# Layer 0 one slot behind its chunk's landing instead of two, in a fused two-layer graph network

## The reference, cut to what matters

```
o = sum over v in 1..3 of (adj == v) @ (x @ w_v);  x = layernorm(x + o + bias)
h = x @ W.T + b;  e = leaky_relu(h @ we1 + be1 + (h @ we2 + be2).T, 0.01)
attention = softmax(where(adj > 0, e, -9e15), axis=1)
x = layernorm(x + attention @ h)
```

## Time and profile before

| | |
|---|---|
| median of 3 | 1608.69 us |
| the profiled execution | 1608.2 us |
| its span | 1606.5 us |
| its mean granted TensorE clock | 0.969 |
| VectorE, ScalarE busy | 1088.5, 979.4 us |

### The profile page before, as it was taken

How to read it: one execution, slowest core, us unless ns; L and a number is a source line. 1 busy time by engine, 2 the same in 40 slices (tenths; PEclk the granted TensorE clock), 3 DMA queues, 4 the chain that set the end, 5 groups by cost and what they waited for, 6 DMA issues and landing times.

```text
span 1606.5 us, 19366 instructions
## 1 busy us (share of the span) xinstructions
PE 1435.4 (89%) x6934; PEld 668.8 (42%) x6934; DVE 1088.5 (68%) x2432; ACT 979.4 (61%) x1536; POOL 119.5 (7%) x154
## 2 busy tenths in 40 slices
PE   1747798889999999999999988999999989998996
PEld 0323344344444444444444433444444444444443
DVE  3556677867878968778678665666566766666554
ACT  2223535555556556456555467787787887788674
POOL 3101111110101110100101030000000000000000
PEclk9988899899999999999999998999999999999998
DMA  9999999995889879967969121000000001000100
GB/s 117 125 123 118 126 98 118 112 115 69 97 108 98 98 70 121 86 69 96 84 67 115 13 66 40 8 27 27 27 27 27 27 27 52 28 27 27 34 1 15
DMA packets 124164, 109.60 MB, mean 68 GB/s; under 512 B 4960, under 2 KB 115104, under 8 KB 124064
## 3 DMA queue, kind: packets, MB, share of 16 engines
q0 software_dynamic: 67584, 67.12, 45.7%
q1 hardware_dynamic: 56480, 41.20, 9.1%
HBM read 296.49 MB, written 13.14 MB: 193 GB/s over the span
## 4 chain that ended last, share of the span: by engine, by line
PE 56%; ACT 17%; DVE 12%; DMA 11%; issue 4%; SPq 0%; DVEq 0%; ACTq 0%
PE ps L1208 35%; PE ps L1167 18%; ACT neg_masks L991 13%; DMA edges<-x 7%; DVE neg_masks L597 3%; DVE pos_masks L599 2%; DMA x_rows<-x 2%; PE ps L1176 1%; DMA e_scratch<-e_turned 1%; DMA e_row<-e_scratch 1%; PE ps L1222 1%; DVE tables L660 1%; ACT L1049 1%; PE ps L1188 1%; DVE seen L559 1%
## 5 line engine op out<-in xcount | busy, mean ns | idle before, releaser
L991 ACT ACTIVATE neg_masks<-e_row,cols 128x512 int8<-128x512 f32 x1024 | 640.4, 708 | 176.7 <-PE ps L1208 137.6
L1208 PE MATMUL ps<-pos_masks,tables 128*128 128x512 fp8e4 x2048 | 616.1, 383 | 65.6 <-DVE pos_masks L599 55.7
L1208 PE MATMUL ps<-neg_masks,tables 128*128 128x512 fp8e4 x2048 | 615.2, 382 | 0.0
L1167 PE MATMUL ps<-edge_masks,tables 128*128 128x512 fp8e4 (+1 forms) x2048 | 470.7, 389 | 0.0
L1208 PEld LDWEIGHTS ps<-pos_masks,tables 128*128 128x128 f16 x2048 | 197.1, 98 | 322.4 <-issue 93.3
L597 DVE TENSOR_TENSOR neg_masks<-pos_masks,neg_masks 128x2048 uint16<-128x2048 uint16 x128 | 156.9, 1226 | 241.9 <-ACT neg_masks L991 240.5
L1208 PEld LDWEIGHTS ps<-neg_masks,tables 128*128 128x128 f16 x2048 | 201.7, 98 | 246.8 <-issue 8.8
L1167 PEld LDWEIGHTS ps<-edge_masks,tables 128*128 128x128 f16 x2048 | 203.3, 100 | 238.1 <-issue 22.2
L578 DVE TENSOR_SCALAR edge_masks<-edges 128x512 uint16<-128x512 uint16 x512 | 123.5, 307 | 77.6 <-PE ps L1167 77.6
L982 ACT ACTIVATE edges<-ps 128x1024 uint8<-128x1024 bf16 x64 | 65.0, 1016 | 177.1 <-PE ps L1176 177.1
L599 DVE TENSOR_TENSOR pos_masks<-pos_masks,neg_masks 128x2048 uint16<-128x2048 uint16 x128 | 156.8, 1225 | 4.4
(11 more groups left out here) (128 smaller groups left out, 728.5 us busy)
## 6 DMA issues: line engine op xcount, KB each, us to landing
adj_in<-adj POOLq DMA_DIRECT2D x84, 512.0 KB, 12.0
tables<-adj POOLq DMA_DIRECT2D x28, 512.0 KB, 20.9
e_row<-e_scratch SPq DMA_DIRECT2D x34, 256.0 KB, 4.1
edges<-adj POOLq DMA_DIRECT2D x16, 512.0 KB, 12.0
part_scratch<-a_c_rows SPq DMA_DIRECT2D x18, 256.0 KB, 3.3
part_in<-part_scratch SPq DMA_DIRECT2D x18, 256.0 KB, 3.0
edges<-x SPq DMA_DIRECT2D x8, 512.0 KB, 16.2
x_rows<-x SPq DMA_DIRECT2D x8, 512.0 KB, 4.9
```

What stands on the lines that cost most here:

```text
L991: ins = e.activation(GN[:, n:n + GR].bitcast(I8), e1row[:, q % 2, :], ACT.Sign, bias=t2[:, JC * c + j:JC * c + j + 1])
L1167: ins = e.matmul(ps[:, h, :], v_hl[:, i, JC * c + j, :], U0[:, n:n + GR].bitcast(kind), start=c == 0 and j == 0 and i == 0, stop=c == NCH ...
L1208: ins = e.matmul(z_bank(q, k), tab[:, c, 2 * k + i, j, :], mask[:, n:n + GR].bitcast(F8A), start=first and j == 0 and i == 0, stop=final a ...
```

## The change

START goes from 5 to 4, so every batch sits one slot earlier, and a tail's offsets are one larger in the same slot. TensorE does layer 0 of chunk k-1 in slot k instead of k-2. A batch that isn't fresh comes first in TensorE's slot, a fresh one after layer 0 as before. In VectorE's slot the masks of a batch that isn't fresh stay near the front, the edge masks of chunk k-1 go ahead of packing, and fresh masks go behind it, behind statistics and e_sums. ScalarE's, GpSimd's and SyncE's code isn't edited (but for `fresh`, which moves out of ScalarE's block); what they do in a tail follows the offsets. The tables of parts 4 to 6 (AGAIN, slots 64 to 66 and two behind) keep their slots. There are 148 slots.

```
-START = 5
+START = 4
...
+def fresh(m):
+
+    return SLOTS[m] == NCH * (BATCH[m][1] // 2 + 1) + START
...
-            return [(S, k - 8 * (S + 1)) for S in range(NS) if 0 <= k - 8 * (S + 1) < 8]
+            return [(S, k - 8 * (S + 1) + 1) for S in range(NS) if 0 <= k - 8 * (S + 1) + 1 < 8]
...
                 for m in at(k):
-                    masks(m)
-                    after(m)
+                    if not fresh(m):
+                        masks(m)
+                        after(m)
+                if 1 <= k <= NCH:
+                    split_rest(k - 1)
+                if 1 <= k <= K:
+                    edge_masks(k - 1, 0)
+                    edge_masks(k - 1, 1)
...
-                if 1 <= k <= NCH:
-                    split_rest(k - 1)
                 if k < K:
                     check_and_pack(k)
                 for S, off in tails(k):
                     if off == 2:
                         v_of(S, 1)
-                if 1 <= k <= K:
-                    edge_masks(k - 1, 0)
-                for S, off in tails(k):
-                    if off == 2:
                         statistics(S)
                     if off == 3:
                         e_sums(S)
-                if 1 <= k <= K:
-                    edge_masks(k - 1, 1)
+                for m in at(k):
+                    if fresh(m):
+                        masks(m)
+                        after(m)
...
-                if 2 <= k < K + 2:
-                    layer0(k - 2, 0)
+                for m in at(k):
+                    if not fresh(m):
+                        batch(m)
+                        after(m)
+                if 1 <= k < K + 1:
+                    layer0(k - 1, 0)
                 for S, off in tails(k):
                     if off == 2:
                         o_of(S, 1)
-                if 2 <= k < K + 2:
-                    layer0(k - 2, 1)
+                if 1 <= k < K + 1:
+                    layer0(k - 1, 1)
                 for m in at(k):
-                    batch(m)
-                    after(m)
+                    if fresh(m):
+                        batch(m)
+                        after(m)
```

More of the change, by code:

```diff
@@ L1072, in after @@
                         out_of(q - LOWS)
-            def fresh(m):
-                return SLOTS[m] == NCH * (BATCH[m][1] // 2 + 1) + START
             e.wait_ge(s_const, 1)
```

## The result

The changed kernel takes 1740.68 us (median of 4, 1738.97 to 1742.43) against 1608.98 for the kernel before (1608.07 to 1610.11): a ratio of 1.0818, 95% interval 1.080 to 1.0837. That is 131.7 us slower; 1729 was forecast. The two profiled spans differ by 1737.3 - 1606.5 = 130.8.

The account below looks back on a forecast made before the run. TensorE was taken as the bound, busy 89% of the span and fully from 533 to 881 us, with the head paced by landings. 1608.2 plus 105.4 of waits plus 15 for the clock gave 1729, range 1675 to 1768.

Parts of the forecast that it names:

- slots 14 to 20: Six slots without batch lose 2.3 to 2.5 each or more, fresh slot 20 takes 31.1 against 24.3: 20.4 us.
- The signs named ahead: TensorE idle 4.6 and 2.7 at tails, 2.3 or 6-plus before layer 0; chunk 7 about 145; 116 us window grown to 128.
- The bubble of 2.3: Slots with nothing ahead of layer 0: TensorE idles 2.3 us for turn, evacuation and masks.
- Head: Up to slot 13: layer 0 of chunk 7 at 145.0, chunk 12 and batch 1 done at 239.2 against 221.2; 18.0 us.
- A tail's second slot: Slots 25, 33, 41, 49, 57: batch waits 4.6, turn 1.2, next slot's batch is 2.7 late; 8.5 us per tail.
- Fresh slots: Waits before layer 0 and fresh batch: 10.3+3.7 at slot 28, 9.6 together for super-row 3, 3.6 for super-rows 4 to 6.
- Slots 61 to 72: Eight batches of slots 65 to 72 take 82.4 us against 81.5: a loss of 0.9.
- Clock: Slower TensorE matmuls behind idle cost 15 us, between bounds of below 0 and 52.
- rival 1: Smaller loss: only waits within slots 28 to 60 stay, the head's 38 are won back; 1678 us, 12%.
- Rival 2: Faster: waits at slots 25 to 60 are hidden, work comes one slot of 14.25 sooner; about 1597 us, 5%.
- The third rival: The clock takes more, 52 us, with longer holes from it; 1765 us, 13%.
- The fourth: Landing of x at 141.26 pins the start, the tail comes no sooner, later waits are hidden; 1609 us, 3%.

Follow-up runs that it names:

- the second experiment: The changed kernel with x_and_bias one offset later, at the end of the slot where the kernel before had it: 1730.95 us.
- the first experiment: The changed kernel with the batch's masks ahead of v_of on VectorE in a tail's second slot: 1705.3 us.
- sixth experiment: The changed kernel with AGAIN a slot sooner (63, 64, 65), so the tables of parts 4 to 6 move with the batches: 1736.5 us.
- the nearest version: The changed kernel with masks, bias, fresh gates, x1_of, table products and o_of reordered within their queues, and START = 5: 1654.25 us.

## Why the prediction was right, step by step

The sum against the two traces, after minus before, each over the same work:

| stretch | forecast | idle, measured | all, measured |
|---|---|---|---|
| head to slot 13 | 18.0 | 13.0 | 10.7 |
| slots 14 to 20 | 20.4 | 15.3 | 19.0 |
| slots 21 to 28 | 14.9 | 17.4 | 22.8 |
| slots 29 to 36 | 14.3 | 13.8 | 19.1 |
| slots 37 to 60 | 36.9 | 32.8 | 45.8 |
| slots 61 to 72 | 0.9 | 12.1 | 11.8 |
| last stage | 0 | 1.9 | 1.7 |
| clock, not laid to a stretch | 15 | | in the above |
| sum | 120.4 | 106.3 | 130.8 |

The last column is cut to 0.01 us at the starts of the same instructions, so it is up to 0.3 off the rounded windows shown above; its entries add to 0.1 more by rounding.

The mechanism is the one forecast: waits of TensorE for producers that now stand too close, at the places named. The signs named ahead came out: 4.27 for 4.6 and 2.29 for 2.7 before batches, 2.05 and 5.97 to 10.76 before layer 0, layer 0 of chunk 7 at 144.3, and 131 us for a full window of eight slots where I had 128. That the idle agrees in sum, 106.3 against 105.4, is partly luck. I had some 5 us too much in the head, 5 in slots 14 to 20 and 4 in slots 37 to 60, and 11 too little in slots 61 to 72 and 2.5 in slots 21 to 28.

- **The bubble of 2.3** is 2.05 (slots 14, 15, 16, 23), and 1.94 where a small product stands between.
- **Head.** The mechanism is shown by the second experiment; 144.3 against my 145.0. The size was wrong: layer 0 of chunk 12 and batch 1 were through at 231.7, not 239.2. Of these 7.5 us 0.7 are that start, and 1.4 the gaps of slots 9 to 11 (9.1, not 10.5). The row of the first fresh batch landed 9.8 after e1's turning at 180.0, not 14.6, and the gates started at 192.7, at once behind the table products, where 14.6 would have put them at 194.6: 1.9. The rest I can't place. I don't know why the row was quicker. The DMA share between turning and landing is 1.03 where it was 1.12, and the hold of VectorE isn't needed for it: without the hold, in the second experiment, the row took 9.1. The rule of "DMA: Bandwidth & Descriptors" of the Trainium skill (section "Issuing engines are not separate DMA queues"), for which I had allowed 2 us at the landing of x, changed nothing there: 27.6 us against 27.5. Whether it is what shortened the row no run here shows.
- **A tail's second slot** was forecast at 4.6, 1.2 and 2.7 and measured at 4.27, 1.15 and 2.29; the first experiment shows the cause of the first. With the clock the two slots of a tail take 11 to 12.5 more, where I had 8.5 and some 2.
- **Fresh slots.** 10.3 and 3.7 for slot 28 are 10.76 and 1.28; 5.9 and 3.7 for slot 36 are 5.97 and 0.97; 2.3 and 1.3 for the later ones 2.05 and 1.18. The second wait is smaller because layer 0 ran slower behind the first, 9.26 for 7.07, as the clock's lower bound had allowed.
- **Slots 61 to 72** is the term that was mis-sized most: 0.9 for 11.8. I had counted eight batches in 82.4 by durations at full speed, and had given slot 65, the last tail's second slot, none of the waits that I gave the five others; the waits there are 4.27, 7.51, 3.21, 2.72 and 8.99, in all 26.7 against 11.7 before batches then. Behind 4.27, 7.51 and 8.99 the matmuls also ran slow, behind 3.21 and 2.72 they did not. 4.2 of the difference come from the tables kept in their slots (sixth experiment): with the tail moved forward and these kept, both make their last tables in slot 68, ahead of the gates of slot 69.
- **Clock.** The mean granted clock fell from 0.969 to 0.948. Matmul time grew by 24.5, some 19 of it slower clock by the estimate above, between my 0 and 52 and near my 15. Of "TensorE: Matmul & The Clock Gate" of the Trainium skill (section "What's actually happening") the traces bear out that idle brings the lower level and activity lifts it: behind 4.26 of idle a pair of matmuls takes 1.01, and 0.59 again before the batch ends. That the first stage behind each hole is wholly slow, which I had drawn from it and which the section doesn't say, they do not: in the first experiment slot 34's matmuls take 0.59 a pair behind 1.15 and 2.29 of idle.
- **Rivals.** That the head's loss is won back (rival 1) fell: slots 21 to 36 lost more than forecast, not less. Rival 2, faster by one slot of the serial chain, was to be decided at slot 25: the batch there waited 4.27 for its masks. START = 5 speaks against it too, as it puts the slot back and gains 12.9. The third rival, the clock, holds for some 19 of its 52. The fourth was right that the landing of x pins the head, where layer 0 of chunk 7 starts 6.7 later than before, but it needed the later waits to be hidden, and they are not.

Left open: what part of the last 46 us, by which the nearest version stays behind the kernel before, is the eight slots without a batch (8 times 2.05 plus clock) and what part is the tails' length. A version that fills those slots with batches was not tried.

## What to carry to other kernels

A stage removed from a hand-ordered pipeline frees no time on an engine that is already full; it takes away distance between producer and consumer, and every queue in which a waiting piece stands ahead of a ready one then shows as idle of the full engine. List for each moved piece what stands ahead of it in each in-order queue, and price the wait by the rows: the waits of a tail came within half a us, while whole stretches were off by up to 11 and their sum was right only because such errors cancelled. Don't expect a latency through DMA from one stretch to hold in another (the same row took 14.6 and 9.8 us), and price idle on TensorE with slower matmuls behind it, here about 19 us on 106.

## What the runs showed of the hardware

Short idle, repeated, came with loss of clock. With layer 0 first, a plain slot has 2.05 us of idle; from slot 43 on it takes 16.48 us two times in three and otherwise 18.17, with a layer 0 of 8.77 in place of 7.07, and the mean granted clock of the run is 0.941. The same idle does not always cost the same. With the masks ahead of v_of, the slot behind a tail's second (34, 42, 50, 58) begins behind 2.29 of idle each time and takes 16.7 twice and 18.4 twice. An estimate for such holes is a mean, not a value for one.
